# One product of two weight matrices in place of an output product per batch, in an eight-stage transformer kernel

## The reference, cut to what matters

```
q = x @ Wq + bq
k = x @ Wk + bk
v = x @ Wv + bv
attn = softmax(q @ k.T / sqrt(128))
a = (attn @ v) @ Wo + bo
x = x + a
gates = softmax(x @ Wg + bg)
hmid = relu(x @ W1[e] + b1[e])           # for each of 8 experts e
y = sum over e of gates[e] * (hmid @ W2[e] + b2[e])
return x + y
```

## Time and profile before

| what | value |
|---|---|
| median of 3 runs | 1030.39 us (1029.54 to 1034.29) |
| time of the profiled execution | 1028.6 us |
| span in its trace, first to last instruction | 1026.9 us |
| TensorE, matmuls busy | 930.4 us, 91% of the span |
| TensorE, weight loads busy | 764.3 us, 74% |
| VectorE, ScalarE, GpSimd busy | 622.8, 573.0, 281.7 us |
| granted TensorE clock, mean over the span | 0.964 of full speed |

### The profile page before, as it was taken

The page is one execution under the profiler, slowest core; times in us unless marked ns, Lnnn a source line. Parts: engine busy times, 40 slices in busy tenths (PEclk is TensorE's granted clock), DMA queues, the critical chain, the costliest instruction groups (busy, mean ns, idle before and its releaser), DMA issues.

```text
span 1026.9 us, 20378 instructions
## 1 busy us (share of the span) xinstructions
PE 930.4 (91%) x7937; PEld 764.3 (74%) x7937; DVE 622.8 (61%) x1966; ACT 573.0 (56%) x966; POOL 281.7 (27%) x357
## 2 busy tenths in 40 slices
PE   3677998988999999999999999999999996999960
PEld 2444555555679888989988989889988985889960
DVE  7778786778468657265554546546455665862226
ACT  2287778775886556364464455545455562754420
POOL 6946144310200111021123222022321103147660
PEclk9689999999999999999999999999999998999995
DMA  6334443352970000000000000000000013023318
GB/s 160 122 126 139 149 138 122 111 197 65 231 181 17 1 1 2 1 1 6 16 2 21 1 17 6 2 22 1 22 1 11 12 42 103 19 57 94 86 37 248
DMA packets 85386, 66.47 MB, mean 65 GB/s; under 512 B 8113, under 2 KB 75814, under 8 KB 85290
## 3 DMA queue, kind: packets, MB, share of 16 engines
q1 hardware_dynamic: 80868, 56.87, 19.2%
q0 software_dynamic: 4352, 8.28, 2.5%
q10 hardware_dynamic: 70, 0.02, 0.0%
HBM read 33.82 MB, written 31.59 MB: 64 GB/s over the span
## 4 chain that ended last, share of the span: by engine, by line
PE 75%; ACT 10%; DVE 9%; issue 3%; DMA 1%; POOL 1%; SPq 0%; POOLq 0%; ACTq 0%; DVEq 0%
PE psum L1396 24%; PE psum L1373 18%; PE psum L1228 4%; PE psum L1166 3%; DVE maxes L1739 2%; PE psum L1136 2%; PE psum L1209 2%; ACT big L2293 1%; PE psum L1287 1%; PE psum L1329 1%; PE psum L1307 1%; PE psum L1242 1%; PE psum L1182 1%; PE psum L1448 1%; PE psum L1158 1%
## 5 line engine op out<-in xcount | busy, mean ns | idle before, releaser
L1396 PEld LDWEIGHTS psum<-ew,big 128*128 128x128 f32 x2560 | 315.4, 191 | 20.6 <-ACT big L2293 4.8
L1396 PE MATMUL psum<-ew,big 128*128 128x128 f32 x2560 | 321.9, 276 | 3.4 <-ACT big L2293 2.2
L2293 ACT ACTIVATE big<-psum,cols 128x512 f32<-128x512 f32 x256 | 174.4, 687 | 165.6 <-PE psum L1373 165.0
L1373 PE MATMUL psum<-parts,q_stack 128*128 128x512 f32 x640 | 217.7, 421 | 0.6 <-ACT big L2300 0.5
L1739 DVE TENSOR_REDUCE maxes<-psum 128x4 f32<-128x1024 f32 (+1 forms) x96 | 113.5, 1218 | 20.5 <-PE psum L1182 20.1
L1859 DVE SCALAR_TENSOR_TENSOR hT<-psum,gates,hT 128x128 f32<-128x128 f32 x256 | 71.8, 344 | 89.2 <-PE psum L1396 88.9
L1373 PE MATMUL psum<-parts,k_stack 128*128 128x512 f32 x320 | 125.8, 393 | 0.0
L2560 POOL DMA_INDIRECT routed<-big,slot_i x64 | 62.7, 979 | 228.1 <-DVE slot_i L2048 183.5
L1373 PEld LDWEIGHTS psum<-parts,q_stack 128*128 128x128 f32 x640 | 106.3, 190 | 12.9 <-ACT big L2300 0.7
L2570 POOL DMA_INDIRECT answers<-hT,to x64 | 62.2, 972 | 60.9 <-DVE hT L2067 41.6
L1373 PEld LDWEIGHTS psum<-parts,k_stack 128*128 128x128 f32 x320 | 60.0, 188 | 13.6
(11 more groups left out here) (381 smaller groups left out, 1586.9 us busy)
## 6 DMA issues: line engine op xcount, KB each, us to landing
q_stack<-q_pieces SPq DMA_DIRECT2D x32, 192.0 KB
k_stack<-k_pieces SPq DMA_DIRECT2D x32, 192.0 KB
routed<-empty_row SPq DMA_DIRECT2D x4, 1040.0 KB, 11.9
big<-routed SPq DMA_DIRECT2D x16, 260.0 KB, 2.9
answers<-gb_tok SPq DMA_DIRECT2D x4, 1024.0 KB, 10.5
q_pieces<-gb_tok SPq DMA_DIRECT2D x16, 192.0 KB, 2.1
k_pieces<-gb_tok SPq DMA_DIRECT2D x16, 192.0 KB, 2.1
x<-in_L_attn_x SPq DMA_DIRECT2D x4, 512.0 KB, 5.9
```

Source lines behind the costliest of these rows:

```text
L1373: last = eng.matmul(bank(i), w1_part(wp, e)[:, fs], parts[2 * xk + xp][:, :], start=n == 0, stop=n == 2)
L1396: last = eng.matmul(psum[:, i, k * C:(k + 1) * C], hid[:, r, f, k * P:(k + 1) * P], ew2[:, e, f, :], start=f == 0, stop=f == FC - 1)
L2293: eng.activation(hid[:, held("hid", "up", n, e, f), f, :], bank(held("bank", "up", n, e, f)), ACT.Relu, bias=col("L0_ffn_b1", e * FC + f)) ...
```

## The change

A new pair of steps runs once. `vo_t` transposes Wv on TensorE, and ScalarE copies it to a tile. `vo` multiplies it with Wo (one matmul of 128 columns) and `L0_ffn_bv` with Wo (one matmul of one column); VectorE copies the product over Wv in `fw[:, 2, :]` and adds `L0_ffn_bo` to the column, into `mixed_bias`. Then `mx_v` makes values that already hold the output matrix, without a bias; `mx_a` writes the final result into PSUM, and VectorE adds `mixed_bias` and the hidden state from there, as `mx_o` did before. The step `mx_o` is gone, and with it one matmul and one ScalarE copy for each batch, and one tile of the five that a batch took. `L0_ffn_bv` moves from the rows (SyncE's queue) to the columns (ScalarE's queue). All that waited for `mx_o` waits for `mx_a`. The diff, without the many places that only swap the name:

```
-        kq, kv, kp, kt, ka = (p.buffer("tmp") for _ in range(5))
+        kq, kv, kp, kt = (p.buffer("tmp") for _ in range(4))
...
-        one("mx_v", b, "pe:.44 dve:.35", [("ln_t", 0, 1, b), ("mx_k", b)], rank, chain, kv)
+        one("mx_v", b, "pe:.44 dve:.35", [("ln_t", 0, 1, b), ("mx_k", b), ("vo",)], rank, chain, kv)
...
-        one("mx_a", b, "pe:.87 act:.33", [("mx_t", b), ("mx_v", b)], rank, chain, ka, [kt, kv], src=kt, val=kv)
-        one("mx_o", b, "pe:.43 dve:.4", [("mx_a", b)] + values_over + ([last_pv] if b >= 4 else []), rank, chain, None, [ka],
-            src=ka)
+        one("mx_a", b, "pe:.87 dve:.4", [("mx_t", b), ("mx_v", b)] + values_over + ([last_pv] if b >= 4 else []), rank, chain,
+            None, [kt, kv], src=kt, val=kv)
...
+    tile = p.buffer("tmp")
+    bank = p.buffer("bank")
+    p.step("vo_t", work="pe:.15 act:.3", after=[("late",)], rank=100, opens=[(0, bank), (0, tile)], closes=[(1, bank)], bank=bank, tmp=tile)
+    bank = p.buffer("bank")
+    p.step("vo", work="pe:.5 dve:.5", after=[("vo_t",), ("cols",)], rank=100, opens=[(0, bank)], closes=[(0, tile), (1, bank)], bank=bank,
+           src=tile)
...
-                        ("L0_ffn_bk", 1), ("L0_ffn_bo", 1), ("L1_attn_p1_b", 1), ("L1_attn_p2_b", 1),
+                        ("L0_ffn_bk", 1), ("L0_ffn_bo", 1), ("L0_ffn_bv", 1), ("L1_attn_p1_b", 1), ("L1_attn_p2_b", 1),
...
-                        ("L0_attn_g_w2", GW), ("L0_attn_g_b2", 1), ("L0_ffn_bv", C), ("L0_ffn_bg", NE),
+                        ("L0_attn_g_w2", GW), ("L0_attn_g_b2", 1), ("L0_ffn_bg", NE),
...
             def mx_v(b):
                 i = held("bank", "mx_v", b)
                 w.wait_ge(*done("ln_t", 0, 1, b))
+                w.wait_ge(*done("vo"))
...
+            def vo_t():
+                i = held("bank", "vo_t")
+                w.wait_ge(late_in, 16 * 8)
+                for c in cleared("bank", "vo_t"):
+                    w.wait_ge(*c)
+                eng.transpose(psum[:, i, 0:C], fw[:, 2, :], ident[:, :]).then_inc(sem("vo_t", "pe"))
+
+            def vo():
+                i = held("bank", "vo")
+                w.wait_ge(*done("vo_t"))
+                w.wait_ge(*done("cols"))
+                for c in cleared("bank", "vo"):
+                    w.wait_ge(*c)
+                eng.matmul(psum[:, i, 0:C], T(held("src", "vo"))[:, 0:C], fw[:, 3, :], start=True, stop=True)
+                eng.matmul(psum[:, i, C:C + 1], fw[:, 3, :], col("L0_ffn_bv"), start=True, stop=True).then_inc(sem("vo", "pe"))
...
-                eng.tensor_tensor(vt, psum[:, held("bank", "mx_v", b), 0:TPB * C].rearrange("p (t c) -> p t c", c=C),
-                                  row("L0_ffn_bv").unsqueeze(1).to_broadcast([P, TPB, C]), ALU.add).then_inc(sem("mx_v"), 1)
+                eng.tensor_copy(vt, psum[:, held("bank", "mx_v", b), 0:TPB * C].rearrange(
+                    "p (t c) -> p t c", c=C)).then_inc(sem("mx_v"), 1)
...
+            def vo():
+                i = held("bank", "vo")
+                w.wait_ge(*done("vo", by="pe"))
+                eng.tensor_copy(fw[:, 2, :], psum[:, i, 0:C])
+                eng.tensor_tensor(mixed_bias[:, :], psum[:, i, C:C + 1], col("L0_ffn_bo"), ALU.add).then_inc(sem("vo"), 1)
...
+                eng.scalar_tensor_tensor(xpT[:, bs], psum[:, held("bank", "mx_a", b), 0:S], mixed_bias[:, :], hT[:, bs],
+                                         ALU.add, ALU.add).then_inc(sem("mx_a"), 1)
...
-            def mx_a(b):
-                w.wait_ge(*done("mx_a", b, by="pe"))
-                for c in cleared("tmp", "mx_a", b):
-                    w.wait_ge(*c)
-                eng.copy(T(held("tmp", "mx_a", b))[:, 0:S], psum[:, held("bank", "mx_a", b), 0:S]).then_inc(sem("mx_a"), 1)
+            def vo_t():
+                w.wait_ge(*done("vo_t", by="pe"))
+                for c in cleared("tmp", "vo_t"):
+                    w.wait_ge(*c)
+                eng.copy(T(held("tmp", "vo_t"))[:, 0:C], psum[:, held("bank", "vo_t"), 0:C]).then_inc(sem("vo_t"), 1)
```

More of the change, by code:

```diff
@@ L103 @@
     "mx_k": ("mix", "pe act"), "mx_v": ("mix", "pe dve"), "mx_s": ("mix", "pe dve"), "mx_e": ("mix", "act"),
-    "mx_n": ("mix", "dve"), "mx_t": ("mix", "pe act"), "mx_a": ("mix", "pe act"), "mx_o": ("mix", "pe dve"),
+    "mx_n": ("mix", "dve"), "mx_t": ("mix", "pe act"), "mx_a": ("mix", "pe dve"), "vo_t": ("fold", "pe act"), "vo": ("fold", "pe dve"),
     "mg_l": ("gates", "pe dve"), "mg_e": ("gates", "act"), "mg_n": ("gates", "dve"),
@@ L503, in add_mixed @@
         tile = p.buffer("tmp")
-        p.step("am_s", n, work="pool:2.4", after=[("mx_o", b) for b in range(BPC * n, BPC * n + BPC)], rank=rank, chain=chain,
+        p.step("am_s", n, work="pool:2.4", after=[("mx_a", b) for b in range(BPC * n, BPC * n + BPC)], rank=rank, chain=chain,
                opens=[(0, tile)], tmp=tile)
         one("am_x", n, "pe:.44 dve:.62", [("am_s", n)], rank, chain, None, [tile], src=tile)
+    tile = p.buffer("tmp")
[4 more added lines that the diff above has]
+           src=tile)
     MOE = 2000
@@ L530, in order_steps @@
         split = p.buffer("parts")
-        p.step("sx", n, work="act:.53 dve:.62", after=[("mx_o", b) for b in range(BPC * n, BPC * n + BPC)]
+        p.step("sx", n, work="act:.53 dve:.62", after=[("mx_a", b) for b in range(BPC * n, BPC * n + BPC)]
                + ([(("up", n - 1, NE - 3, FC - 1), "pe")] if n else []),
@@ L779, in build @@
         magic = sb("magic", [P, 1])
+        mixed_bias = sb("mixed_bias", [P, 1])
         least = sb("least", [P, 1])
@@ L1345, in mg_l @@
                     t = g * LG + m
-                    w.wait_ge(*done("mx_o", t // TPB))
+                    w.wait_ge(*done("mx_a", t // TPB))
                     last = eng.matmul(psum[:, i, m * NE:(m + 1) * NE], xpT[:, t * P:(t + 1) * P], wg[:, :],
@@ L1549, in _ @@
                     "exp": exp, "pv": pv, "turn": turn, "po_t": po_t, "po_w": po_w, "po_x": po_x, "am_x": am_x,
-                    "mx_k": mx_k, "mx_v": mx_v, "mx_s": mx_s, "mx_t": mx_t, "mx_a": mx_a, "mx_o": mx_o, "mg_l": mg_l,
+                    "mx_k": mx_k, "mx_v": mx_v, "mx_s": mx_s, "mx_t": mx_t, "mx_a": mx_a, "vo_t": vo_t, "vo": vo, "mg_l": mg_l,
                     "ss_t": ss_t, "ss_b": ss_b, "up": up, "down": down, "sg_m": sg_m, "wt": wt, "la_q": la_q,
@@ L1813, in mx_o @@
                     w.wait_ge(*done("pv", B - 1, 5))
-                eng.scalar_tensor_tensor(xpT[:, bs], psum[:, held("bank", "mx_o", b), 0:S], col("L0_ffn_bo"), hT[:, bs],
-                                         ALU.add, ALU.add).then_inc(sem("mx_o"), 1)
+                eng.scalar_tensor_tensor(xpT[:, bs], psum[:, held("bank", "mx_a", b), 0:S], mixed_bias[:, :], hT[:, bs],
+                                         ALU.add, ALU.add).then_inc(sem("mx_a"), 1)
             def mg_l(g):
@@ L2266, in ss_b @@
                 for b in range(BPC * n, BPC * n + BPC):
-                    w.wait_ge(*done("mx_o", b))
+                    w.wait_ge(*done("mx_a", b))
                 eng.copy(hT[:, n * CHUNK:(n + 1) * CHUNK], bank(held("bank", "ss_b", n))).then_inc(sem("ss_b"), 1)
```

15 lines of the change are left out of this document (5 added, 10 removed).

## The result

Measured side by side on one chip, 22 executions each, the kernel before takes 1031.53 us (median) and the changed kernel 1028.24 us: a ratio of 0.9972, 95% interval 0.996 to 0.9984. That is 2.9 us faster (0.28%), within the 0.5% that the prediction set as the border of no change. Forecast were 1023.6 us and 6.8 us. The profiled execution spans 1025.0 us, before 1026.9.

What follows compares the result with a forecast made beforehand. TensorE was taken to bound the kernel from about 253 to 850 us. The terms -7.3 + 0.5 + 0 = -6.8 us, taken from the median of 1030.39 us, gave 1023.6 us, range 1018.4 to 1030.9 us.

Steps and rivals of the forecast that it cites:

- What bounds the kernel: From about 253 to 850 us the time is TensorE's work laid end to end; all removed work lies in its part.
- Removed from TensorE, -7.3 us: 16 `mx_o` matmuls gone from the stretch TensorE bounds: between 6.9 and 8.0 us, taken as 7.3 us.
- The dense rate: Lower bound for the removed matmuls: 0.43 us each from start to next start, 16 x 0.43 = 6.9 us.
- Added, +0.5 us: The pair `vo_t`, `vo` in the causal attention's head, about 50 to 60 us: 0 to 1.3 us, taken as 0.5.
- DMAs, 0: One more issue on ScalarE's queue (0.36 us, hidden), one fewer on SyncE's (0.43 us, not waited for): nothing.
- The removed work in full: In the full TensorE stretch, matmuls busy 112.00 of 112 us: all 7.3 us removed counted in the forecast time.
- The order at 0, with a bound of 4 us: The planner's new order on every engine: value 0, bounded by a fifth of TensorE's 20 us of gaps, 60 to 250 us.
- keeps its length: Sign to look for: the exit at 850 to 905 us stays as long as before.
- The signs of being wrong: Causal attention's end moves over 3 us, the experts' stretch gets new gaps at ScalarE, or TensorE waits for `vo`.
- the order gives a part back: Rival: causal attention or the exit at 850 us gets 2 to 6 us longer, giving 1027.6 us; chance 0.22.
- Row maxima exposed: Rival: TensorE waits 4.25 us per batch for maxima issued just ahead of `exp`, giving 1036.4 us; chance 0.07, 0.05 slower.
- The clock: Rival: wider gaps at 850 to 905 or 60 to 250 us lower TensorE's clock, 3.3 us, 1026.9 us; chance 0.05.

Runs made afterwards that it cites:

- e1: Kernel before, every engine keeping its order, but without each batch's `mx_o` matmul and ScalarE copy and without the product of the two weight matrices: 0.9961 to the kernel before.
- e13: Whole change, everything computed, pair planned at rank 600 so every engine keeps before's order: 0.9955 to the kernel before, 1054.99 us.
- e2: Changed kernel in its own order, with the pair `vo_t`, `vo` in the plan but issuing nothing: 0.9982 to the kernel before.
- e15: Kernel before with only the free copy: fills take zeros from another tile, so ScalarE's first copy into `gb_tok` doesn't wait for them: 0.9997 to the kernel before.
- e4: Kernel before with all output matmuls kept and the pair `vo_t`, `vo` added at rank 100, its result unused: 1.0068 to the kernel before.
- e16: Changed kernel itself, timed again as a yardstick on the slower chip: 1.0029 to the kernel before, 1063.48 us.
- e3: Changed kernel in its own order, with one unread f32 matmul of 256 columns put back into each batch's `mx_a`: 1.0033 to the kernel before.

## Why the prediction was wrong

**What bounds the kernel: right in the main.** The stretch from 300 to 850 us stays full and at clock 1.00, and TensorE's busy time ahead of the last `ag` falls in e1 and in e13. The stretch from the first `mx_k` to the last sum became 6.3 us shorter (158.8 to 152.5), where about 7 were forecast, but not "at equal fullness": it has 3.7 us of gaps instead of 0.65.

**Removed from TensorE, -7.3 us: right in kind, too high.** Behind 60 us busy time falls by 5.7 us in e1 and by 5.2 in e13, which has the pair in it; putting the work back cost 5.3 to 6.3 us. The dense rate, 6.9 us, was the better end, and still lies above all of these. Nor did this work arrive in full as time, and that is one of the two steps that failed (below).

**Added, +0.5 us: not measurable.** In e2 no cost of its work shows; `vo_t` was at 52.7 us, without a wait for its weights, and the last `exp` moved by 1.2 us where under 1 was said.

**DMAs, 0: right for the two that were moved.** The fills, which the sum doesn't name, are the transfers that mattered.

**Two steps failed: the removed work was let through in full, and the order was put at 0.**

*The removed work in full.* I took a stretch whose matmuls are busy for 112.00 of 112 us to mean that every microsecond taken out of it shows at the end. With before's order held it doesn't: at the last `ag` 3.6 us of 5.7 are there in e1, and 3.7 of 5.2 in e13. TensorE comes earlier to waits that the removed step had covered: from 280 to 440 us they are 3.2 us in e1 (2.4 for the copy behind the fills) and 2.5 us in e13 (1.2 for that copy), against 0.4 us before and in e15. Together with the too high price this leaves 4.0 us by the ratio of e1 and 4.8 by that of e13, instead of 6.8.

*The order at 0, with a bound of 4 us.* I bounded it by a fifth of the gaps between 60 and 250 us. Runs show that it can be as large as the gain: +7 us in e4 for half a microsecond of work, 7.8 us between e13 and e16 for the same work. It acts where I hadn't looked. The first place is the tail, of which the forecast said that its first part, 850 to 905 us, "keeps its length". With the new tail it is 5.9 us longer on the first chip, 1.6 to 3.5 us on the second (e2, e3 against e1, e4) and 4.3 to 7.9 us on the slower ones. The second is 285 to 310 us, where the fills set a landing time that moves with the last maxima and not with TensorE.

On the two chips near 1030 us, one of which gave the result and the other e1, the first step weighs more than the second. Of the 3.9 us that are missing from 6.8, before's order in e1 already misses 2.8; the new order adds 1.1 (0.9961 to 0.9972), which the intervals don't tell from nothing. There the order moves much in both directions, 4.2 us earlier at the last `ag` and 4.8 us longer behind it than in e1, and the two nearly cancel, which is luck. On the slower chip of e13 to e16 they don't.

The signs of being wrong that the prediction named: the causal attention's end moved by 0.9 us, under its 3, and TensorE never waited for `vo`; but a new gap behind ScalarE did appear, the 2.38 us at 297.62 us. The chances don't add up as stated: by their parts faster is 0.63, within 0.5% 0.32 and slower 0.05, not 0.62, 0.31 and 0.07.

In the profiled pair of the first chip the 1.9 us between the spans are -7.8 us at the last `ag` and +5.9 us behind it. The rival "the order gives a part back" (1027.6 us, measured 1028.2) names the right place, the exit, and nearly the time; that before's order gives a good part back as well it doesn't say. **Row maxima exposed** didn't happen to `exp`, but its cause did: the last maxima moved by 2.8 us in the changed kernel and by 5.4 in e4, and what waited was the fills' copy. **The clock** is part of the tail's loss: 0.66 to 0.52 in the first ten microseconds, 1.6 us of 5.9.

**Open.** On the slower chips the changed kernel loses its lead at the last `ag`: from first to last `ag` it needs 442.6 us (e16) against 434.4 (e13), while on the first chip it needs 429.8 against 428.8 before. TensorE is busy for 423.6 us of it in e16 and for 419.7 in e13, and idle for 19.0 and 14.8; the waits that the trace names are 11.9 and 9.9 us of that, so most of the 8 us I can't place. Nor do I know what makes these chips slower. Which steps of the tail's new order cost how much wasn't tried one by one.

## What to carry to other kernels

Where a planner writes the order, a change of the arithmetic is two changes: measure the new work in the old order first (here 0.9955), then the new order (1.0029), and keep the better. The first of the two was also the steadier: 0.9961 (e1, without the product) and 0.9955 (e13) on two chips, where the new order gave 0.9972, 1.003 and 1.0029. An order that was tuned is tuned to the work in it: a step that is removed may have covered a wait, so count a removed step at its price less the waits that it filled (here about two thirds of the price were left). Before crediting a gain upstream, look for landings that don't move with the engine that gets faster, such as a transfer queued behind some other chain that an in-order engine must pass.

## What I had not expected of the hardware

Behind idle gaps of the same length TensorE stayed at its 1.2 GHz level for different times. Stretches of one microsecond, columns as above; before, where work starts again at 868.27 us:

```profile
870.00:871.00 1.00, 1.00 (x7) 0.50 0.25 58
871.00:872.00 1.00, 1.00 (x6) 0.86 0.00 0
```

The changed kernel, where work starts again at 860.47 us:

```profile
865.00:866.00 1.00, 1.00 (x4) 0.50 0.00 0
866.00:867.00 1.00, 1.00 (x5) 0.64 0.00 0
```

The full level is back 3.0 us behind the first gap and 6.2 us behind the second. Before, the four transposes of `ln_t` alternate with eight of `ft` without a break; after, four transposes are followed by a second, short break (0.86 us of work from 861 to 862 us) and then by the products. Whether it is the break or the kind of the matmuls wasn't tried.

One kernel differs by 3% between chips, and its rival may differ by another amount: the changed kernel has 0.9972 on one and 1.003 and 1.0029 on two others. On the chip of e13 to e16 TensorE has a pause at 930 to 950 us in the tail that the first chip doesn't show: 6.1 us and then 3.4 us in e13, 4.7 us and then 1.7 us in e16. In 20 us of it the kernel of e13 works for less than half:

```profile
927.00:947.00 20.00, 9.12 (x40) 0.66 0.17 51
```

The kernel before has no such gap on the first chip (rows of its tail above). With the free copy it has it on this one (e15: 6.1 and 3.4 us); there TensorE waits for ScalarE and VectorE, and what these wait for, 6.7 and 11.4 us, the trace doesn't name.
